# Conditions read in one packet, whole-bank moves, and stores split by partition half over two queues

## What is computed

```python
w = weights[conditions]                        # (128, 64, 64)
return x + jnp.einsum('bct,bcd->bdt', x, w)    # (128, 64, 512)
```

## Time and profile before

| | value |
|---|---|
| median of 3 runs | 53.17 us |
| the profiled execution | 52.95 us |
| its span, first to last instruction | 51.1 us |
| HBM read, written | 9.47 MB, 8.39 MB |
| busy: PE, DVE, ACT | 18.1, 27.3, 19.9 us |

### The profile page before, as it was taken

The page is one execution under the profiler, slowest core; times in us unless marked ns, Lnnn a source line. Parts: engine busy times, 40 slices in busy tenths (PEclk is TensorE's granted clock), DMA queues, the critical chain, the costliest instruction groups (busy, mean ns, idle before and its releaser), DMA issues.

```text
span 51.1 us, 425 instructions
## 1 busy us (share of the span) xinstructions
PE 18.1 (36%) x128; PEld 6.3 (12%) x128; DVE 27.3 (53%) x44; ACT 19.9 (39%) x33; POOL 1.3 (2%) x5
## 2 busy tenths in 40 slices
PE   0000000000000000599999777897777760000000
PEld 0000000000000000233444221222322200000000
DVE  1000130000001899408999999999999999991000
ACT  0900000000000000008899999999999875000000
POOL 1000035000000000000000000000000000000000
PEclk9999999999999999999999999999999999855555
DMA  0025999999999999999999999999999999999940
GB/s 0 7 53 189 356 401 404 400 387 436 395 390 393 388 385 385 387 390 387 385 387 390 408 406 411 404 409 409 404 404 408 406 409 403 401 404 398 392 185 37
DMA packets 8992, 17.86 MB, mean 350 GB/s; under 512 B 672, under 2 KB 672, under 8 KB 8864
## 3 DMA queue, kind: packets, MB, share of 16 engines
q1 hardware_dynamic: 8704, 16.78, 86.8%
q0 software_dynamic: 144, 1.05, 5.0%
q10 hardware_dynamic: 144, 0.03, 0.3%
HBM read 9.47 MB, written 8.39 MB: 350 GB/s over the span
## 4 chain that ended last, share of the span: by engine, by line
DVE 50%; DMA 18%; issue 15%; PE 4%; DVEq 1%; POOLq 0%
DVE y_sb L138 42%; DMA gathered<-weights,table_row 18%; DVE w_all L132 7%; PE product L107 4%; DVE gathered L130 1%; DVEq L34 1%; POOLq L34 0%; POOLq L147 0%
## 5 line engine op out<-in xcount | busy, mean ns | idle before, releaser
L86 ACT COPY y_sb<-product 64x512 f32<-64x512 f32 x32 | 18.6, 580 | 21.8 <-PE product L107 21.0
L107 PE MATMUL product<-x_sb,w_all 64*64 64x512 f32 x128 | 18.1, 671 | 23.5 <-DVE w_all L132 21.0
L138 DVE COPY y_sb<-product 64x512 f32<-64x512 f32 x32 | 22.1, 689 | 3.1 <-PE product L107 2.1
L107 PEld LDWEIGHTS product<-x_sb,w_all 64*64 64x64 f32 x128 | 6.3, 208 | 34.5 <-DVE w_all L132 21.0
L130 DVE TENSOR_SCALAR gathered<-gathered 32x32 f32<-32x32 f32 x4 | 0.7, 187 | 9.6 <-DMA gathered<-weights,table_row 9.5
L132 DVE STREAM_TRANSPOSE w_all<-gathered 128x2048 f32<-128x2048 f32 x1 | 3.6, 3622 | 0.0
L118 DVE STREAM_TRANSPOSE condition_of<-condition 64x32 int32<-64x32 int32 x2 | 0.4, 206 | 5.0 <-DMA condition<-conditions 5.0
L86 ACT ACT_TABLE_LOAD x1 | 1.3, 1283 | 1.2 <-PEq L147 1.2
L92 POOL DMA_INDIRECT gathered<-weights,table_row x1 | 1.1, 1068 | 6.8 <-DVE table_row L122 6.8
L114 DVE MEMSET piece<- 32x1 f32 x4 | 0.2, 59 | 1.0 <-PEq L147 0.8
L122 DVE TENSOR_SCALAR table_row<-condition_of,piece 128x1 int32<-128x1 int32 x1 | 0.2, 212 | 0.1
## 6 DMA issues: line engine op xcount, KB each, us to landing
x_sb<-x SPq DMA_DIRECT2D x16, 512.0 KB, 11.5
out<-y_sb SPq DMA_DIRECT2D x16, 512.0 KB, 5.1
condition<-conditions ACTq DMA_DIRECT2D x1, 32.0 KB, 5.4
gathered<-weights,table_row POOLq DMA_INDIRECT x1, 9.2
```

The lines of the kernel that those rows point to most:

```text
L86: nc.scalar.copy(y_sb[halves(0), 2 * m + g, :], product[m % SETS][0][halves(g), :]).then_inc(moved_by_act, 1)
L107: product_of = nc.tensor.matmul(product[m % SETS][h][halves(g), :], w_all[halves(h), :, n], x_sb[halves(h), n, :], start=True, stop=True)
L138: nc.vector.tensor_copy(y_sb[halves(1), 2 * m + g, :], product[m % SETS][1][halves(g), :]).then_inc(moved_by_dve, 1)
```

## The change

- The conditions are loaded as one run of 256 bytes to partition 0 (`condition[0:1]`). `condition` now has 32 rows, which VectorE clears first; ScalarE's queue waits for that before it issues the load. The turning is done by four transposes of 32x32 instead of two of 64x32.
- The diagonal is added by one tensor_tensor over 128 partitions, with a `piece` of two columns (1 - piece, piece), half of which GpSimd sets. It replaces four tensor_scalar.
- Rounds are grouped in turns of two (8 turns). `product[set][h]` is now two banks, 1024 columns, and there are two sets. A move covers 128 partitions and 1024 columns without changing partitions: one for each engine and turn.
- `y_sb` has the layout [g and channel][round][h][time], so that samples 4m and 4m+1 are on the lower partition half and 4m+2 and 4m+3 on the upper one. A round is stored by two DMAs of 256 KB and 64 partitions: the lower half from SP, the upper from ScalarE's queue. ScalarE issues the upper stores of a turn four turns later (`LAG = 4`), and the first of them waits for the last load of x.

```diff
-    out_rows = out.rearrange("(n two) c t -> (two c) n t", two=PAIR)
+    out_rows = [out.rearrange("(m g h) c t -> g c m h t", g=2, h=PAIR)[g] for g in range(2)]
...
-                sp.wait_ge(moved_by_act, 2 * (m + 1))
-                sp.wait_ge(moved_by_dve, 2 * (m + 1))
-                sp.dma_start(out_rows[:, 2 * m:2 * m + 2, :], y_sb[:, 2 * m:2 * m + 2, :]).then_inc(stored, 16)
-            sp.wait_ge(stored, 16 * ROUNDS)
+                if m % 2 == 0:
+                    sp.wait_ge(moved_by_act, m // 2 + 1)
+                    sp.wait_ge(moved_by_dve, m // 2 + 1)
+                sp.dma_start(out_rows[0][:, m, :, :], y_sb[halves(0), m, :, :]).then_inc(stored, 16)
+            sp.wait_ge(stored, 16 * 2 * ROUNDS)
...
-            act.dma_start(condition[:, :], condition_row.to_broadcast([P, B])).then_inc(condition_loaded, 16)
-            for m in range(ROUNDS):
-                act.wait_ge(multiplied, m + 1)
-                for g in range(2):
-                    nc.scalar.copy(y_sb[halves(0), 2 * m + g, :], product[m % SETS][0][halves(g), :]
-                                   ).then_inc(moved_by_act, 1)
+            def store_upper(turn):
+                if turn == 0:
...
+                    act.wait_ge(x_loaded[ROUNDS - 1], 16)
+                act.wait_ge(moved_by_act, turn + 1)
+                act.wait_ge(moved_by_dve, turn + 1)
+                for m in range(2 * turn, 2 * turn + 2):
+                    act.dma_start(out_rows[1][:, m, :, :], y_sb[halves(1), m, :, :]).then_inc(stored, 16)
...
+            act.wait_ge(condition_cleared, 1)
+            act.dma_start(condition[0:1, :], condition_row).then_inc(condition_loaded, 16)
+            for turn in range(TURNS):
+                if turn >= LAG:
+                    store_upper(turn - LAG)
+                act.wait_ge(multiplied, turn + 1)
+                nc.scalar.copy(y_sb[:, 2 * turn:2 * turn + 2, 0, :], product[turn % SETS][0][:, :, :]
+                               ).then_inc(moved_by_act, 1)
+            for turn in range(TURNS - LAG, TURNS):
+                store_upper(turn)
...
-            for q in range(P // Q):
...
-                first = (q % K) * Q
-                diagonal = gathered[q * Q:(q + 1) * Q, first:first + (Q - 1) * (D + 1) + 1:D + 1]
-                nc.vector.tensor_scalar(diagonal, diagonal, 1.0, None, ALU.add).then_inc(identity_added, 1)
-            dve.wait_ge(identity_added, P // Q)
+            diagonal = bass.AP(gathered, 0, [[Q * D, P], [D + 1, Q], [Q, K]])
+            nc.vector.tensor_tensor(diagonal, diagonal, piece[:, :].unsqueeze(1).to_broadcast([P, Q, K]), ALU.add
+                                    ).then_inc(identity_added, 1)
```

More of the change, by code:

```diff
@@ L48, in conditioned_residual_kernel @@
         w_all = sbuf("w_all", [P, D, PAIRS], fp32)
-        product = [[ctx.enter_context(nc.psum_tensor(f"product{s}_{h}", [P, T], fp32)) for h in range(PAIR)]
+        product = [[ctx.enter_context(nc.psum_tensor(f"product{s}_{h}", [P, 2, T], fp32)) for h in range(PAIR)]
                    for s in range(SETS)]
@@ L98, in _ @@
             pe.wait_ge(w_ready, 1)
[L99 to L108, removed]
+            for turn in range(TURNS):
+                if turn >= SETS:
+                    pe.wait_ge(moved_by_act, turn - SETS + 1)
+                    pe.wait_ge(moved_by_dve, turn - SETS + 1)
+                for j in range(2):
+                    pe.wait_ge(x_loaded[2 * turn + j], 16)
+                    for g in range(2):
+                        for h in range(PAIR):
+                            n = 4 * turn + 2 * j + g
+                            product_of = nc.tensor.matmul(product[turn % SETS][h][halves(g), j, :],
+                                                          w_all[halves(h), :, n], x_sb[halves(h), n, :],
+                                                          start=True, stop=True)
                 product_of.then_inc(multiplied, 1)
@@ L112, in _ @@
         def _(dve):
+            nc.vector.memset(condition[:, :], 0).then_inc(condition_cleared, 1)
             for q in range(P // Q):
-                nc.vector.memset(piece[q * Q:(q + 1) * Q, :], float(q % K)).then_inc(pieces_set, 1)
+                nc.vector.memset(piece[q * Q:(q + 1) * Q, 1:2], float(q % K)).then_inc(pieces_set, 1)
             dve.wait_ge(condition_loaded, 16)
-            for h in range(PAIR):
-                nc.vector.transpose(condition_of[halves(h), :], condition[halves(h), h:B:PAIR]
+            for q in range(P // Q):
+                nc.vector.transpose(condition_of[q * Q:(q + 1) * Q, :], condition[:, q // K:B:PAIR]
@@ L132, in _ @@
+            dve.wait_ge(identity_added, 1)
             nc.vector.transpose(w_all[:, :, :], gathered[:, :].rearrange("p (c d) -> p d c", d=D)
                                 ).then_inc(w_ready, 1)
[L135 to L139, removed]
+            for turn in range(TURNS):
+                dve.wait_ge(multiplied, turn + 1)
+                nc.vector.tensor_copy(y_sb[:, 2 * turn:2 * turn + 2, 1, :], product[turn % SETS][1][:, :, :]
+                                      ).then_inc(moved_by_dve, 1)
```

19 lines of the change are left out of this document (12 added, 7 removed).

## The result

| | before | changed |
|---|---|---|
| median | 53.28 us (4 runs) | 56.26 us (4 runs, 55.69 to 56.91) |
| ratio | 1 | 1.053, interval 1.043 to 1.064 |
| profiled execution, its span | 52.95, 51.1 us | 56.36, 54.6 us |
| busy: PE, DVE, ACT | 18.1, 27.3, 19.9 us | 16.0, 15.0, 9.4 us |

The changed kernel is slower by 5%, though VectorE works little more than half as long and ScalarE less than half. The forecast was 52.1 us, faster than before. The time lies within 0.1 us of the upper end of the range (56.3), on the side of the first rival.

What follows compares the result with a forecast made beforehand. The DMA engines were taken to bound the kernel, with a store backlog to the end. 52.95 us (profiled) - 1.0 (earlier start) + 0 (moves, head, waits) = 51.95, stated as 52.1 us; range 51.2 to 56.3.

Steps and rivals of the forecast that it cites:

- first rival: Stores: one partition half alone runs at half rate, 203 GB/s, at both ends; 3.4 us more, 55.4 us; chance 33%.
- The DMA engines set the time: Whole kernel: a store backlog stands to the end, so larger moves are worth nothing in the time.
- The head: Start: x's bytes up to 1.2 us earlier, gain 1.0 us (bounds 0 and 2.2); weights ready at 18.3 us, hidden.
- The stores: 32 stores of 256 KB for 16 of 512 KB: 0 us, if halves pass at full rate, mixed or alone.
- The second rival: Stores: engines take the same half at once throughout, 203 GB/s, 72.6 us; partial overlap from 57 up; chance 8%.
- The third: Rival at the start: the condition load was not in x's way, x starts at 3.0 us, time 53.0; chance 13%.
- The wait of ScalarE's queue for the last load: First upper store waits, holding up copies: costs nothing, issues 0.42 us each, all moved by 36 us, at worst 41.
- theory A: Experiments' theory: partitions touched set a transfer's rate, one half reaching half the paths; 0.77 us per us of one half alone.

Runs made afterwards that it cites:

- first kernel of rates: Only stores, nothing computed, seven stages one after another: 128 partitions 379 GB/s, partitions 0 to 63 211, 32 to 95 382, both halves from two queues 348.
- cond_only: The kernel before with the conditions loaded in one run, the diagonal still in four instructions: 51.24 us against 53.13, ratio 0.960.
- head_only: The kernel before with the changed head alone (conditions in one run, diagonal in one instruction): 51.88 us, ratio 0.973; timed again 51.26 us, ratio 0.962.

## Why the prediction was wrong, step by step

- **The DMA engines set the time: right.** Larger moves gave nothing beside the head (51.32 and 51.26 us). The changed kernel doesn't show it by itself, since its stores slowed at the same time.
- **The head: right in mechanism, undersized.** The conditions were there at 2.7 us (4 expected), the gather began at 4.2 (5.2), and the weights were ready at 17.9 (18.3). The terms as written give the gather at 5.5 and not 5.2 (4 + 1.04 + 0.47), and the 1.5 us from landing to gather are what was measured; nothing hangs on it. x's first bytes came at 1.8 us, and 3 to 6 us had 301 GB/s (over 280 expected). The step was priced at 1.0 us; alone it measured 1.2 us in four runs and 1.9 in six later ones, within the bounds of 0 and 2.2; why the two differ is not known.
- **The stores: here it failed.** The step was "It costs nothing as long as lower and upper stores pass at full rate, mixed or alone. I take that as the likeliest, since nothing in the trace shows a rate that depends on partitions." The trace of before had no transfer by which it could have been seen. Measured: 0 to 63 alone 211, 32 to 95 382, both halves 348 GB/s. From silence I took the end of the bounds at which nothing changes, and put the stores at 0 us, against the first rival, for which the prediction itself had cited the Trainium skill. The new layout and stores cost 4.4 to 5.0 us (56.26 against 51.88 and 51.26 with the head alone).
- **The first rival: right in mechanism and place, mis-sized in one term.** Upper stores alone at the end at half rate, 3.4 us expected and some 5 us seen; lower stores alone after the loads, only partly slow (386 GB/s in 27 to 30 us, then 306). The term that was missing is the one between: "then both halves flow at 405, 7.0 MB in 17.3 us". At 342 GB/s the same bytes take 20.5 us, 3.2 us more. What it gave too much at the start, and too little to the head, makes up for part of this, so that its 55.4 us came only 0.9 us short of 56.26. That the time fell just inside the range is in part luck. That the middle stretch is slow because the halves collide rests on the 348 GB/s of the first kernel of rates; the 406 of halves in turns behind loads shows that the partitions alone don't fix this rate.
- **The second rival (no overlap, 72.6 us): wrong**, but a partial form of it is the missing 15% of the middle stretch. The prediction let partial overlap begin at 57 us, and gave no working for that; a small loss of overlap costs less, and the measured 56.26 lies below. **The third: wrong**; the condition load was in x's way, as the start with 144 packets and with 2 shows. That their descriptors are made in turn was a guess and stays one; no run tests by what the small load holds up the large one.
- **The wait of ScalarE's queue for the last load: harmless to the supply, as said**, but its issues are not 0.42 us each. Two take 2.1 to 3.5 us, and they stand ahead of the copies of turns 4 to 7. SP's stores too took 1.35 us each to issue in the median, where before they took 0.37. That an issue waits for room in a queue that is full fits this and is not shown. All was moved by 40.9 us (36 expected, 41 at worst), with no gap in the DMA engines' busy share. What the wait costs is the lateness of the second half, 0.77 us for each by theory A.

## What to carry to other kernels

A layout that makes moves cheaper is paid for at the stores if it cuts them into partition halves; ask first whether the moves are on the path at all, and a store backlog says that they are not. When an edit changes the partitions of bulk transfers and the trace has no such transfer, don't price it at the known rate: a small kernel of nothing but these transfers answers it in one run. A tiny load that is spread over all partitions can delay the first large one; one row of 256 bytes was worth 1.2 to 1.9 us.

## What the runs showed of the hardware that I had not expected

- Halves in turns from one queue run at 271 GB/s after a pause and at 406 right behind loads of 128 partitions, for 15 us; lower stores alone keep 405 GB/s for about 2 us behind such loads before they fall to 208; and stores of 128 partitions run at 379 after a pause and at 408 behind loads. None of this is explained.
- A move of 64 partitions and 1024 columns takes as long as one of 128 (1.223 and 1.224 us on VectorE, 1.008 and 1.012 on ScalarE).
- With the quick head, the rate sinks to 164 to 180 GB/s near 5 us, once x has run at 410 for some 2 us (the slices above, and 233 in the page's slices of the changed kernel). The kernel before doesn't show it, and in the profile of `cond_only` the lowest slice has 246. Only SP's queue has packets from 4.2 to 6.3 us of `head_only`, so the gather, issued at 4.5 us, is not yet moving bytes. The dip takes back a part of the gain at the start, and its cause is open.
